# One pass written once and looped, or seven passes written out: the batch loops of a fused recommendation tower

## The reference

```python
xk = x0                                   # (1024, 39, 16)
for W in (f0, f1, f2):                    # 39*39, 128*39, 128*39 rows by 128
    z = einsum('bfd,bgd->bfgd', x0, xk).reshape(b, f * g, d)
    xk = einsum('bpd,pm->bmd', z, W)      # (1024, 128, 16)
    outs.append(xk)
z = sum(concatenate(outs, axis=1), axis=-1)          # (1024, 384)
h = relu(concatenate([z, dense_ctx], 1) @ W_top1 + b_top1)
y = relu(h @ W_top2 + b_top2) @ W_top3               # (1024, 1)
```

## Time and profile before

| | |
|---|---|
| median of 3 executions | 1340.23 us (1337.1 to 1341.92) |
| the profiled execution | 1339.86 us |
| its span, first to last instruction | 1337.7 us |
| mean granted TensorE clock | 0.995 |
| busy: PE, DVE, ACT, POOL | 94%, 79%, 56%, 71% |

### The profile page before, as it was taken

How to read it: one execution, slowest core, us unless ns; L and a number is a source line. 1 busy time by engine, 2 the same in 40 slices (tenths; PEclk the granted TensorE clock), 3 DMA queues, 4 the chain that set the end, 5 groups by cost and what they waited for, 6 DMA issues and landing times.

```text
span 1337.7 us, 25407 instructions
## 1 busy us (share of the span) xinstructions
PE 1261.2 (94%) x5493; PEld 964.8 (72%) x5493; DVE 1056.4 (79%) x3346; ACT 748.6 (56%) x2422; POOL 952.3 (71%) x844
## 2 busy tenths in 40 slices
PE   0799999999999999999999999999999999999999
PEld 0477777777777778677777777777777777877765
DVE  3589996889869997799868998599886898698840
ACT  4356664656546665566645566366654666566641
POOL 6378885788858886688866888578875788666540
PEclk9999999999999999999999999999999999999999
DMA  7532221122222212122211222112221222111000
GB/s 169 151 107 66 66 68 44 42 62 60 59 63 58 57 50 53 47 65 66 66 37 41 60 63 64 51 45 57 64 59 55 66 65 58 43 44 52 3 0 1
DMA packets 121771, 78.48 MB, mean 59 GB/s; under 512 B 77437, under 2 KB 89827, under 8 KB 121653
## 3 DMA queue, kind: packets, MB, share of 16 engines
q1 hardware_dynamic: 106124, 73.45, 19.4%
q0 software_dynamic: 10240, 2.64, 2.3%
q10 hardware_dynamic: 5288, 1.32, 0.5%
HBM read 18.50 MB, written 2.63 MB: 16 GB/s over the span
## 4 chain that ended last, share of the span: by engine, by line
PE 72%; issue 9%; POOL 9%; DVE 5%; ACT 2%; DMA 2%; SPq 1%; POOLq 0%; DVEq 0%; ACTq 0%
PE ps L492 17%; PE ps L496 16%; PE ps L493 16%; PE ps L472 12%; POOL terms L410 6%; PE ps L517 4%; PE ps L508 3%; DVE terms L816 3%; DVE prods_low L788 2%; POOL x_in L386 2%; PE ps L574 2%; ACT terms L661 2%; PE ps L584 1%; DMA w<-in_f 1%; DMA dense_rows<-in_dense_ctx 1%
## 5 line engine op out<-in xcount | busy, mean ns | idle before, releaser
L816 DVE SCALAR_TENSOR_TENSOR terms<-ps,x_scal,terms 128x128 f32<-128x128 f32 x2944 | 807.2, 343 | 192.3 <-ACT terms L661 87.5
L661 ACT ACTIVATE terms<-ps,x_scal 128x128 f32<-128x128 f32 x2048 | 582.9, 368 | 417.3 <-PE ps L496 373.6
L410 POOL TENSOR_TENSOR terms<-terms 128x1024 f32<-128x1024 f32 (+2 forms) x384 | 581.7, 1515 | 217.3 <-DVE terms L816 186.3
L492 PE MATMUL ps<-w_high,x_high 128*128 128x512 f32 (+1 forms) x1280 | 577.2, 451 | 10.7 <-ACT terms L661 7.3
L496 PE MATMUL ps<-w_high,x_low 128*128 128x512 f32 (+1 forms) x1280 | 497.3, 388 | 0.0
L493 PE MATMUL ps<-w_low,x_high 128*128 128x512 f32 (+1 forms) x1280 | 495.7, 387 | 0.0
L386 POOL DMA_INDIRECT x_in<-in_tables,row_at x320 | 305.6, 955 | 89.0 <-issue 85.5
L492 PEld LDWEIGHTS ps<-w_high,x_high 128*128 128x128 f32 x1280 | 241.8, 189 | 92.0 <-issue 28.7
L493 PEld LDWEIGHTS ps<-w_low,x_high 128*128 128x128 f32 x1280 | 242.3, 189 | 76.3 <-issue 29.8
L496 PEld LDWEIGHTS ps<-w_high,x_low 128*128 128x128 f32 x1280 | 241.3, 189 | 51.0
L472 PE MATMUL ps<-prods,w 117*128 117x512 f32 x262 | 135.4, 602 | 13.4 <-issue 13.4
(11 more groups left out here) (48 smaller groups left out, 380.1 us busy)
## 6 DMA issues: line engine op xcount, KB each, us to landing
prods<-x_cols SPq DMA_DIRECT2D x190, 234.0 KB
x_cols<-x_rows SPq DMA_DIRECT2D x93, 78.0 KB
x_first<-x_cols SPq DMA_DIRECT2D x93, 78.0 KB
x_in<-in_tables,row_at POOLq DMA_INDIRECT x320
x_diag<-x_scal SPq DMA_DIRECT2D x256, 9.8 KB
s<-in_f SPq DMA_DIRECT2D x3, 832.0 KB
x_rows<-x_in SPq DMA_DIRECT2D x31, 80.0 KB
wt<-in_W_top SPq DMA_DIRECT2D x1, 768.0 KB
```

The costliest lines, as they stand in the source:

```text
L410: nc.gpsimd.tensor_tensor(t[:, 0:n], t[:, 0:n], t[:, n:2 * n], ALU.add).then_inc(s_tree, 1)
L492: nc.tensor.matmul(y, x1_high[:, par, at:at + P], high, start=True, stop=False)
L661: op = nc.scalar.activation(terms[:, u % 2, FB * ACT_BANKS.index(q) + i, :], ps[:, (BANKS * u + q) % RING, i * G:(i + 1) * G], ACT.Copy, s ...
L816: nc.vector.scalar_tensor_tensor(out=acc, in0=y, scalar=x0, in1=acc, op0=ALU.mult, op1=ALU.add).then_inc(s_mac, 1)
```

## The change

The loops become Python loops that write every pass out. All seven (SyncE: six) passes stand one after another in each engine's program, every wait compares with a constant, and three slices with a register start (`bass.ds`) become plain slices. The work, its order on each engine, the buffers and the semaphores are the same.

```diff
@@ prologue_then_batches (tensor, scalar, vector)
-            with eng.Fori(0, NBATCH - 1) as bt:
+            for bt in range(NBATCH - 1):
                 for u in range(2, STEPS + 2):
                     step(bt, u, False)
@@ sync
-            with sp.Fori(1, NBATCH - 1) as bt:
+            for bt in range(1, NBATCH - 1):
                 load_ids(bt + 1)
@@ gpsimd
-            with pool.Fori(0, NBATCH - 1) as bt:
+            for bt in range(NBATCH - 1):
                 for u in range(STEPS):
@@ store_r (scalar)
-                nc.scalar.activation(r2[:, bass.ds(bt * BATCH, BATCH)], s3[:, F, :], ACT.Copy).then_inc(s_r, 1)
+                nc.scalar.activation(r2[:, bt * BATCH:(bt + 1) * BATCH], s3[:, F, :], ACT.Copy).then_inc(s_r, 1)
@@
-                nc.scalar.activation(r3[:, bass.ds(bt * BATCH, BATCH)], ps[:, S3_BANK, R3_AT:R3_AT + BATCH],
+                nc.scalar.activation(r3[:, bt * BATCH:(bt + 1) * BATCH], ps[:, S3_BANK, R3_AT:R3_AT + BATCH],
@@ split_x1 (vector)
-                nc.vector.tensor_reduce(r1[:, bass.ds(gf * (GCOLS // D), GCOLS // D)],
+                nc.vector.tensor_reduce(r1[:, gf * (GCOLS // D):(gf + 1) * (GCOLS // D)],
```

## The result

The changed kernel takes 1308.39 us (median, 1307.54 to 1308.95), the kernel before in the same comparison 1339.16 us (1337.1 to 1341.92). The ratio is 0.977, 95% interval 0.975 to 0.979. The forecast was 1316 us with a range of 1308 to 1326. The direction and the main mechanism were right. The size was not: the time lies 0.4 us inside the range and outside the 1311 to 1321 us that the forecast had for itself. The profiled execution took 1308.95 us, 30.9 us less than that of before.

The account below looks back on a forecast made before the run. PE, busy nearly throughout, was taken as the bound, so only time in which it stands could be gained: 1339.86 - 20.9 (branches) - 3 (GpSimd's registers) = 1316 us, range 1308 to 1326.

Parts of the forecast that it names:

- The branches of ScalarE and VectorE: Third step, six batches behind a branch back: 74.10 us become 53.16, gain 20.9 us, low bound 14.8.
- The reading of the pause as a fetch: At the loop branch, DVE's 2.8 and ACT's 3.5 us pauses are the fetch of the loop's start.
- The register arithmetic of PE, ACT and DVE: It goes, but is hidden beside the matmuls, as in the fourth step; gain nothing.
- rival A: Only the branches pay, L788 waits as before; 1319 us, 0.70 together with the forecast.
- The register arithmetic of GpSimd, seventh step: POOL's chain is 0.15 us a step shorter, so L788 waits less in seven batches; 3 us, bounds nothing to 8.9.
- in this stretch it runs without a pause over three steps: POOL before the seventh step: 0.15 us saved a step, so L788 waits some 0.4 us less.
- The rest is in pieces below a microsecond each: PE's 5.61 us of standing outside the second step: 3.04 in the third, 1.39 in the seventh, the rest scattered.
- Longer code: Each engine fetches its whole program once; PE's stream is the new case, costed at nothing, some 43 q8 packets.
- Rival D: PE stands for each of 31 more instruction packets, 34 us; 1353 us, chance 0.04.
- E: The pause is a fetch at a code edge, branch or not, and every pass keeps it; 1339 us, chance 0.03.
- B: L788 and GpSimd's adds in the seventh step come apart altogether, all 8.9 us gained; 1310 us, chance 0.12.
- C: New collisions: one more L788 a batch falls into a large add, +8.9 us; 1325 or 1328 us, chance 0.11.

Follow-up runs that it names:

- e3: Only ScalarE's loop written out, against the kernel before; 1318.82 us, ratio 0.984.
- e5: Kernel before with all loops kept; ScalarE's loop turned so its branch comes just before its wait for the third layer; 1317.13 us, ratio 0.984.
- e6: Against the kernel before: TensorE and GpSimd loop over two batches a pass, ScalarE and VectorE are written out; 1317.33 us, ratio 0.984.
- e10: e5 with GpSimd written out, its row numbers after its adds, and TensorE's wait for third-layer weights at first use in each pass; 1297.4 us, ratio 0.968.
- e9: Changed kernel with GpSimd's row numbers after its adds and TensorE's wait for third-layer weights at their first use; 1296.9 us, ratio 0.968.
- e2: Only GpSimd's loop written out, against the kernel before; 1330.87 us, ratio 0.992.
- e1: Loops of TensorE, ScalarE and VectorE written out, GpSimd and SyncE keep theirs, against the kernel before; 1316.28 us, ratio 0.982.
- e4: Only VectorE's loop written out, against the kernel before; 1331.83 us, ratio 0.995.

## Why the prediction was right, and where it fell short

- **The branches of ScalarE and VectorE.** Right: 20.9 us forecast, 20.9 measured in the same six steps. The model for it, the last batch's third step at 8.86 us, was matched to 0.04 us. e3 and e5 add what the prediction did not say: it is ScalarE's branch that counts. The low clock of two of the steps (0.76 and 0.87) went with the pause, as the 20.9 us had it: it is 1.00 in all six.
- **The reading of the pause as a fetch.** It held: e6 makes the pause appear on the two engines that didn't have it (3.9 and 2.7 us for 0.3), by nothing but a longer body, and q8 has 40 packets in the stretch where it had none. Over all runs 2.4 to 3.9 us stood between a branch back to a long body and the next sequencer instruction.
- **The register arithmetic of PE, ACT and DVE.** Right: e10 has it all (1297.4 us) and is level with e9 (1296.9). The records show the arithmetic and that it went. At L815, VectorE's wait for `s_mac`, the kernel before has 2345 ALU_OP and 7 FUSED_REGOPS records of DVEq (40 and 46 ns at the median, the last at 1164.4 us, ahead of the last branch at 1164.7) and 80 EVENT_SEMAPHORE records, 5 a step in the 16 steps outside its loop; the changed kernel has 640 EVENT_SEMAPHORE records there (21 ns) and no others. What rival A had for itself is there too: at L406, GpSimd's second wait of two ahead of its adds, the changed kernel keeps an EVENT_SEMAPHORE record in each of the 128 steps (17 ns), where the kernel before has 105 ALU_OP (32 ns), 7 FUSED_REGOPS and 16 EVENT_SEMAPHORE records. So the instruction for the wait stayed and the arithmetic went.
- **The register arithmetic of GpSimd, seventh step.** The mechanism was right, the size was not. I took 3 us; it was 1.8, and 2.6 in e2. That "in this stretch it runs without a pause over three steps" was a wrong reading: in the kernel before, GpSimd waits there for the last gather to land, for 1.52 us before its L381. In the changed kernel that wait is 1.58 us in the second batch, whose seventh step takes 9.58 us, but longer in the sixth, whose seventh step takes 10.24:

```profile
861.39 0.27 POOL L381 TENSOR_TENSOR row_at<-ids_now,ids_base 128x40 uint32<-128x40 uint32 x1 [2.22 <-DMA x_in<-in_tables,row_at]
```

- **The fifteenth step.** The step of the sum that failed is "The rest is in pieces below a microsecond each", which put them at nothing. One of these pieces is the fifteenth step, 0.9 us in six batches. It has the same L788 beside the same adds, and its first batch had it at 8.90 us, so the row that would have told was in the trace. It gave 5.7 us, most of the 7.6 us by which the forecast was too high. That GpSimd's loop holds it long is shown (e1, e2). That its register arithmetic does is not: see e6.
- **Longer code.** Right: q8 has 44 packets in all (43 forecast), and the steps that PE fills are as long as before. Rival D fell. So did E, by the 0.48 us above.
- **Rivals B and C.** B's time, 1310, was the nearest, by another way: 1.8 of the seventh step's 8.9 us came, but a collision that I hadn't counted went. So the low end of the range held the result by luck, since it had been drawn for B. C's sign showed without its price: the fourteenth step took up a longer L788 (1.06 us) without being longer.
- **The start.** 1.3 us are from there. Its second and third step change length from kernel to kernel (12.6 and 10.9 us in the changed kernel, 9.5 and 9.1 before, 13.9 and 10.2 in e6), with the landing of the weights: PE's stand on that DMA is 4.33 us in the changed kernel, 2.31 in e1 and 5.60 in e6. In the other kernels that keep this wait the fourth step starts between 75.3 and 77.8 us, against 77.15 in the changed kernel and 78.40 before. So 1.3 us is no more than what the start varies by, and not shown to come from the change.
- **Open:** why ScalarE's pause is shorter in e4, and what the gap before GpSimd's twelfth L414 is.

## What to carry to other kernels

In these runs a hardware loop cost at its branch where its body was long (a pause of 2.4 to 3.9 us, against about 0.3), and only as far as the engine had work due there (11.2 us and more for the third step in the kernel before, 8.9 in e5): look for the idle time right behind each branch, engine by engine, and turn the loop so that the branch comes before a long wait. Constants in place of registers gained nothing on TensorE, VectorE and ScalarE (e9 1296.9 us, e10 1297.4). On GpSimd a tenth of a microsecond, whatever it came from (0.26 us idle before an add in e1, 0.16 in e6), decided which of two engines had to wait, and with it 0.9 us of the next step. When a batch is cut into steps for a forecast, the repeated pieces below a microsecond belong in the sum: six times 0.9 us here, with the same instruction in them as the one that was costed.

## What the runs showed of the hardware

- A taken branch of a loop cost 2.4 to 3.9 us to the next sequencer instruction where the body was long, on four engines, and 0.2 to 0.3 us where it was short. ScalarE paused with 423 recorded instructions in a pass, VectorE with 892. GpSimd changed from one to the other between 210 and 418 recorded instructions in a pass (the kernel before and e6), TensorE between one batch a pass and two. With its one-batch body the queue q8 carried nothing for 964 us; in e6, with the two-batch body, it carried 40 packets between 221 and 1150 us.
- VectorE's L788 took 0.68 us alone and up to 2.07 us when a GpSimd add was under way (e1). In the kernel before, each of the 40 of its 93 that took over 0.75 us had such an add beside it. The other way round GpSimd's three adds grew from 4.6 to 5.06 us. Which of them waited went with which had started first, to about a tenth of a microsecond: an add that started 0.08 us ahead of L788 still gave way, one that started 0.20 us ahead did not.
- After PE had stood, the granted clock read 0.50 for part of the step in some cases (0.50 over 700 to 706 us in the kernel before, 65 to 71 us in the changed one and 878 to 881 us in e1): after 1.79 us in a seventh step of e1 (mean clock 0.86), after stands of 2.54 us in all in a third step of the kernel before (0.76), and after 4.33 us in the second step of the changed kernel (0.77 in the third). In others it did not: a third step of the kernel before with 3.04 us of stand kept 1.00.
